# First cross attention of a decoder kernel: value products with queries on partitions, sums in two columns of ones, division there, weighted rows turned on TensorE

## The reference, cut to what matters

```python
def proj(x, W):
    return (x @ W.T).reshape(b, -1, HEADS, D_K).transpose(0, 2, 1, 3)
qh, kh, vh = (proj(q, Wq), proj(k, Wk), proj(v, Wv))
att = jnp.einsum('bhqd,bhkd->bhqk', qh, kh) / jnp.sqrt(jnp.float32(D_K))
att = jnp.where(mask, NEG, att)
att = jax.nn.softmax(att, axis=-1)
out = jnp.einsum('bhqk,bhkd->bhqd', att, vh)
out = out.transpose(0, 2, 1, 3).reshape(b, -1, D_MODEL)
return out @ Wo.T
```

## Time and profile before

| | us |
|---|---|
| median of 3 runs | 2332.08 (2328.46 to 2333.09) |
| profiled execution | 2333.0 |
| its span | 2331.2 |
| mean granted TensorE clock | 0.955 |
| TensorE matmul busy | 2144.7 (92%) |
| TensorE weight load busy | 1749.1 (75%) |
| VectorE busy | 1134.2 (49%) |
| ScalarE busy | 974.6 (42%) |
| POOL busy | 662.4 (28%) |

### The profile page before, as it was taken

One profiled execution on the slowest core, in us unless ns is written; L12 is line 12 of the kernel. 1 busy time (PEld: TensorE's weight loads), 2 busy tenths in 40 slices (PEclk: granted clock), 3 DMA queues, 4 the chain that ended last, 5 costly groups with the idle time before them and its releaser, 6 DMA issues. The chain is left out here.

```text
span 2331.2 us, 41914 instructions
## 1 busy us (share of the span) xinstructions
PE 2144.7 (92%) x13788; PEld 1749.1 (75%) x13789; DVE 1134.2 (49%) x3298; ACT 974.6 (42%) x1907; POOL 662.4 (28%) x889
## 2 busy tenths in 40 slices
PE   7997898779999789999998699889999999999998
PEld 5664455468999656666665477789899999999997
DVE  4543786755333477777765255354222222222245
ACT  2221564343444345555555233301455555555310
POOL 1111777662601234444422122127000000000063
PEclk9997999889999969999999799799999999999999
DMA  9940000033222322222221100155111111011033
GB/s 310 386 158 1 1 1 28 23 101 116 71 70 86 86 92 92 93 93 92 92 74 38 57 4 5 61 193 174 36 34 34 35 32 36 32 36 32 28 116 100
DMA packets 153119, 183.46 MB, mean 79 GB/s; under 512 B 27602, under 2 KB 121362, under 8 KB 152850
## 3 DMA queue, kind: packets, MB, share of 16 engines
q1 hardware_dynamic: 137730, 145.34, 19.2%
q0 software_dynamic: 12288, 33.57, 4.6%
q10 hardware_dynamic: 2960, 2.75, 0.5%
HBM read 73.34 MB, written 74.19 MB: 63 GB/s over the span
## 5 line engine op out<-in xcount | busy, mean ns | idle before, releaser
L2578 DVE CUSTOM_DVE_ANT_0 a_s_ps<-a_s_ps,a_causal 128x512 f32<-128x512 f32 (+3 forms) x512 | 242.2, 512 | 118.0 <-PE a_s_ps L2368 116.3
L2501 ACT ACTIVATE a_prob<-a_st_ps 128x512 f32<-128x512 f32 (+1 forms) x384 | 197.1, 526 | 200.3 <-PE a_st_ps L2384 195.1
L2024 PE MATMUL e_up_ps<-e_xT,e_ring 128*128 128x128 f32 x2272 | 276.7, 275 | 0.0
L2024 PEld LDWEIGHTS e_up_ps<-e_xT,e_ring 128*128 128x128 f32 x2272 | 270.7, 192 | 3.8
L1976 POOL DMA_INDIRECT e_wgu<-slots_y,slot x64 | 61.2, 957 | 620.3 <-DMA slots_y<-e_y 575.8
L2059 ACT ACTIVATE e_hT<-e_up_ps 128x512 f32<-128x512 f32 x103 | 61.5, 597 | 370.5 <-PE e_y_ps L2034 363.0
L2054 ACT ACTIVATE e_ring<-e_wgu 128x512 f32 (+2 forms) x355 | 180.8, 531 | 77.6 <-PE e_up_ps L2024 75.9
L2034 PE MATMUL e_y_ps<-e_wd,e_hT 128*128 x852 | 195.7, 379 | 0.0
L2384 PE MATMUL a_st_ps<-rf_qs,a_ks 128*128 128x512 f32 (+3 forms) x512 | 179.6, 394 | 4.7 <-DMA rf_qs<-a_m_lo 3.2
L2368 PE MATMUL a_s_ps<-a_ks,rf_qs 68*128 68x512 f32 (+3 forms) x512 | 158.3, 354 | 24.0 <-DVE a_most L2578 23.3
L2292 POOL TENSOR_SCALAR_AFFINE_SELECT a_prob<-a_prob 128x256 f32<-128x256 f32 x256 | 98.5, 410 | 285.9 <-ACT a_prob L2501 285.7
(11 more groups left out here) (453 smaller groups left out, 4041.8 us busy)
## 6 DMA issues: line engine op xcount, KB each, us to landing
slots_x<-zero_row SPq DMA_DIRECT2D x4, 8448.0 KB, 50.0
e_xin<-slots_x SPq DMA_DIRECT2D x142, 128.0 KB, 2.0
rf_qs<-late_w SPq DMA_DIRECT2D x128, 128.0 KB, 2.4
a_ks<-late_w SPq DMA_DIRECT2D x120, 128.0 KB, 2.3
slots_x<-e_y SPq DMA_DIRECT2D x71, 128.0 KB, 1.7
slots_y<-e_y SPq DMA_DIRECT2D x71, 128.0 KB, 1.7
e_wgu<-in_L_ffn_wg SPq DMA_DIRECT2D x8, 688.0 KB, 9.8
e_wgu<-in_L_ffn_wu SPq DMA_DIRECT2D x8, 688.0 KB, 11.2
```

The costliest lines, as they stand in the source:

```text
L2024: last = pe.matmul(up_ps[:, j, bank, (first + n) * P:(first + n + 1) * P], weights, xT[:, j, k * P:(k + 1) * P], start=k == 0, stop=k == K ...
L2501: act.activation(prob[:, n % 2, u // 3, (u % 3) * BANK:(u % 3) * BANK + cols], st_ps[:, u % 2, 0:cols], ACT.Exp).then_inc(exp_done, 1)
L2578: last = dve.tensor_tensor_reduce(s_ps[:, u % 2, off:off + cols], s_ps[:, u % 2, off:off + cols], causal[:, S - cols:], 1.0, -3.0e38, ALU. ...
```

## The change

The value products change sides. The turned probabilities of a pair of heads (128 keys by 128 queries) are held in the array, and `vblk` moves: 32 columns of values and two more, one column of ones for each head of the pair (zeros at the other head's keys). The result has queries on partitions, and for each pair 32 weighted values and 2 sums. VectorE takes the reciprocal of the 16 sums and multiplies the 256 values by them (`shared`). TensorE then transposes the 256 columns in two pieces (`turn_out`), ScalarE copies them as before, and the projection follows. Gone are the sum over the probabilities (L1178) and POOL's pass over them (L931); `turn_probs` waits for the exponentials alone. The projection is a step later, of tile i - 5, and stands ahead of the turning of probabilities; on VectorE the maximum stands ahead of `shared(i - 4)` and the addition to x. POOL sets the columns of ones once.

The diff, with a few declarations left out:

```diff
@@ sizes and buffers
-        o_half = lambda i: out_bank[:, 0, 0:D].rearrange("p (k q) -> p k q", k=KT)
+        PAIR = 2 * HD + 2
+        o_pairs = out_bank[:, 0, 0:PAIRS * PAIR].rearrange("p (n c) -> p n c", n=PAIRS)
         w_half = lambda i: out_bank[:, 1, 0:D]
+        turned_half = out_bank[:, 1, D:2 * D]
-        vblk = sb("vblk", [P, 2, PAIRS, 2 * HD])
+        vblk = sb("vblk", [P, 2, PAIRS, PAIR])
+        share = sb("share", [P, 2, PAIRS, 2])
+        o_rows = sb("o_rows", [P, 2, D])
@@ POOL
-            def normalise(i):
-                pool.wait_ge(share_done, i + 1)
-                pool.tensor_tensor(heads(i), heads(i), share[:, i % RING].unsqueeze(2).broadcast_to([P, HEADS, SC]),
-                                   ALU.mult).then_inc(prob_done, 1)
+            pool.memset(vblk[:, :, :, 2 * HD:PAIR], 0.0).then_inc(ones_ready, 1)
+            pool.wait_ge(ones_ready, 1)
+            pool.memset(vblk[0:SC, :, :, 2 * HD:2 * HD + 1], 1.0).then_inc(ones_ready, 1)
+            pool.wait_ge(ones_ready, 2)
+            pool.memset(vblk[SC:P, :, :, 2 * HD + 1:PAIR], 1.0).then_inc(ones_ready, 1)
+            pool.wait_ge(ones_ready, 3)
             for i in range(STEPS):
                 if tile(i):
                     subtract(i)
-                if tile(i - 1):
-                    normalise(i - 1)
@@ TensorE
             def turn_probs(i):
-                pe.wait_ge(prob_done, i + 1)
+                pe.wait_ge(exp_done, i + 1)
...
             def weighted(i):
                 pe.wait_ge(p_kept, i + 1)
                 pe.wait_ge(v_kept, i // TB + 1)
-                after(pe, o_kept, i)
+                after(pe, o_shared, i)
+                if i == 0:
+                    pe.wait_ge(ones_ready, 3)
                 for n in range(PAIRS):
-                    r = 2 * HD * (n % 4)
-                    last = pe.matmul(o_half(i)[r:r + 2 * HD, n // 4, :], vblk[:, i // TB % 2, n, :], probT[:, i % 2, n, :], start=True, stop=True)
+                    last = pe.matmul(o_pairs[:, n, :], probT[:, i % 2, n, :], vblk[:, i // TB % 2, n, :], start=True, stop=True)
                 last.then_inc(o_done, 1)
+
+            def turn_out(i):
+                pe.wait_ge(o_shared, i + 1)
+                after(pe, x_done, i)
+                for k in range(KT):
+                    last = pe.transpose(turned_half[:, k * P:(k + 1) * P], o_rows[:, i % 2, k * P:(k + 1) * P], g.ident[:, :])
+                last.then_inc(o_turned, 1)

             def project_out(i):
                 pe.wait_ge(o_kept, i + 1)
-                after(pe, x_done, i)
@@ TensorE's loop
                 if tile(i + 1):
                     scores(i + 1)
+                if tile(i - 5):
+                    project_out(i - 5)
                 if tile(i - 2):
                     turn_probs(i - 2)
...
                 if tile(i - 3):
                     weighted(i - 3)
                 if tile(i - 4):
-                    project_out(i - 4)
+                    turn_out(i - 4)
...
+            project_out(NT - 1)
@@ ScalarE
             def keep_weighted(i):
-                act.wait_ge(o_done, i + 1)
-                after(act, w_done, i - 1)
-                act.activation(oT[:, i % 2], o_half(i), ACT.Copy).then_inc(o_kept, 1)
+                act.wait_ge(o_turned, i + 1)
+                act.activation(oT[:, i % 2], turned_half.rearrange("p (k q) -> p k q", k=KT), ACT.Copy).then_inc(o_kept, 1)
-                if tile(i - 3):
-                    keep_weighted(i - 3)
+                if tile(i - 4):
+                    keep_weighted(i - 4)
@@ VectorE
-            def shares(i):
-                dve.wait_ge(exp_done, i + 1)
-                dve.tensor_reduce(total[:, i % RING], heads(i), AX.X, ALU.add).then_inc(sum_done, 1)
-                dve.wait_ge(sum_done, i + 1)
-                after(dve, prob_done, i + 1 - RING)
-                dve.reciprocal(share[:, i % RING], total[:, i % RING]).then_inc(share_done, 1)
+            def shared(i):
+                dve.wait_ge(o_done, i + 1)
+                dve.reciprocal(share[:, i % 2], o_pairs[:, :, 2 * HD:PAIR]).then_inc(share_done, 1)
+                dve.wait_ge(share_done, i + 1)
+                after(dve, o_turned, i - 1)
+                dve.tensor_tensor(o_rows[:, i % 2].rearrange("p (n a c) -> p n a c", n=PAIRS, a=2),
+                                  o_pairs[:, :, 0:2 * HD].rearrange("p n (a c) -> p n a c", a=2),
+                                  share[:, i % 2].unsqueeze(3).broadcast_to([P, PAIRS, 2, HD]), ALU.mult).then_inc(o_shared, 1)
@@ VectorE's loop
                 if tile(i):
                     masked(i)
+                if tile(i):
+                    maximum(i)
+                if tile(i - 4):
+                    shared(i - 4)
                 if tile(i - 5):
                     add_to_x(i - 5)
-                if tile(i):
-                    maximum(i)
...
-                if tile(i - 1):
-                    shares(i - 1)
```

More of the change, by code:

```diff
@@ L840, in l0_cross_attention @@
         gate, gate_bias, sorted_ = routing.gate, routing.gate_bias, routing.sorted
-        most, total, share = (sb(n, [P, RING, HEADS]) for n in ("most", "total", "share"))
+        most = sb("most", [P, RING, HEADS])
+        share = sb("share", [P, 2, PAIRS, 2])
+        o_rows = sb("o_rows", [P, 2, D])
         probT = sb("probT", [P, 2, PAIRS, P])
@@ L1185, in keep_value @@
                 after(dve, o_done, (c - 1) * TB)
-                dve.tensor_tensor(vblk[:, c % 2], seq_bank[:, 0:D].rearrange("p (n c) -> p n c", n=PAIRS),
+                dve.tensor_tensor(vblk[:, c % 2, :, 0:2 * HD], seq_bank[:, 0:D].rearrange("p (n c) -> p n c", n=PAIRS),
                                   head_of_key[:, :].unsqueeze(1).broadcast_to([P, PAIRS, 2 * HD]), ALU.mult).then_inc(v_kept, 1)
```

5 lines of the change are left out of this document (3 added, 2 removed).

## The result

| | before | after |
|---|---|---|
| median (executions) | 2330.59 (6) | 2352.39 (6) |
| lowest to highest | 2322.82 to 2333.09 | 2342.61 to 2355.43 |
| profiled execution, its span | 2333.0, 2331.2 | 2353.8, 2351.6 |
| stage, from the start of step 0 to its last row | 268.3 | 288.4 |

The changed kernel is slower: the ratio is 1.0092, with a 95% interval of 1.0068 to 1.0115. The forecast was 2351.0, within 2338 to 2366.

A forecast was written before the change was run, and what follows sets the result against it. TensorE's queue was taken as the bound in steps 4 to 19, POOL in 20 to 26, VectorE's routing chain at the end. Eight window terms summed to +19.2 us on the median 2332.08, giving 2351, range 2338 to 2366.

The forecast's parts named there:

- The price of the products: Value products on TensorE: sixteen instructions with 128 columns held take 1.70 us instead of 0.58, +1.12 us a tile.
- A microsecond added to it there is a microsecond of the span: Steps 4 to 19: TensorE is the bound as a queue of work, so work added there lengthens the span equally.
- Steps 4 to 7: Window of four loop steps: 25.35 us goes to 30.4, with waits left in its first and last step; +5.1 us.
- Steps 8 to 11 and 20 to 23: Two windows: 5.4 us more TensorE work each, plus waits; in the second, POOL waits mostly go; +4.9 and +2.3 us.
- Steps 12 to 15: Window of four loop steps: 25.35 us plus 5.4 of work and 1.4 of waits make 32.1; +5.8 us.
- The halved clock behind that wait stays: Steps 16 to 19: TensorE's half clock behind the routing count's wait was to remain; the window was put at +4.7 us.
- POOL's bound in steps 20 to 26: POOL is the bound there, one tile taking 7.5 us; without the dividing pass, steps 24 to 27 shorten by 4.3 us.
- Two sums leave that chain early: Steps 28 to 35, set by VectorE's routing chain: 2.7 us leave it, 2.3 come back at the end; -0.4 us.
- Faster: Rival: dividing pass and sum were the bound, new products cost like today's; -11.7 us, 2320; 7%.
- Half hidden: Rival: VectorE's relief also shortens the end by 6 us, or the half clock doesn't return in count steps; 2341; 11%.
- Dearer products: Rival: each load of 128 columns waits for the 34 moving ones ahead, 14 us; 2365; 7%.
- a new loop: Rival: with one product bank, tile i-3 waits for VectorE's division of tile i-4, 1 us in 25 steps; 2376; 4%.

The follow-up runs named there:

- the twelve transposes: The kernel before with 12 transposes of the identity matrix added ahead of each tile's value products, nothing else of the change; 2353.93 us, ratio 1.0104.
- e6: The kernel with both parts: the kernel before without sum, reciprocal and POOL's dividing pass, plus twelve more transposes a tile on TensorE; 2332.2 us, ratio 1.0.
- e2: The kernel before without the sum over the probabilities, its reciprocal and POOL's dividing pass, so weights are not normalised; 2303.46 us, ratio 0.9897.
- e10: The changed kernel with four more identity transposes a tile on TensorE, ahead of the value products; 2361.63 us, ratio 1.0126 to the kernel before.
- e11: e6 with its twelve added transposes replaced by seven products of 34 moving columns (14 instructions); 2347.74 us, ratio 1.0067 to the kernel before.

## Why the prediction was right, point by point

The total was forecast at +19.2 us in the profiled execution and measured at +20.8 (2333.0 to 2353.8), of which the stage is 20.1.

| steps | forecast | measured |
|---|---|---|
| 0 to 3 | +1.1 | +1.0 |
| 4 to 7 | +5.1 | +3.8 |
| 8 to 11 | +4.9 | +4.2 |
| 12 to 15 | +5.8 | +6.8 |
| 16 to 19 | +4.7 | +5.1 |
| 20 to 23 | +2.3 | +1.6 |
| 24 to 27 | -4.3 | -4.4 |
| 28 to 35 | -0.4 | +2.0 |

- **The price of the products** was right: 1.70 us a tile, +1.12, shown by the timeline and, at full clock, by issuing them twice (51.6 us for 54). The transposes took 0.26 instead of 0.22, a term mis-sized by 1 us in all.
- **"A microsecond added to it there is a microsecond of the span"** held to six tenths or more in steps 4 to 19: the twelve transposes, 5.6 us in four steps, gave 4.5, 3.7, 4.8 and 3.5 us. The rest went into the small waits.
- **Steps 4 to 7** were 1.3 us too dear, and 1.0 of it is a slip in the sum. With the projection a step later, this window has three projections and not four (12 instructions of L1059 in the trace, 16 of L1047 before), and the last window has nine and not eight (36 and 32). The forecast added the 0.97 us at the end and did not take it off here.
- **Steps 8 to 11 and 20 to 23** were 0.7 us too dear each. The waits came out as forecast (1.15 us in both, for 1.1 and 1.2). TensorE's busy time grew by 4.7 us instead of 5.4. Why is open.
- **Steps 12 to 15** were 1.0 us too cheap. The row after stands at clock 0.95, 3.3 us at the half clock, which the forecast had at none.
- **Steps 16 to 19** were 0.4 us too cheap. "The halved clock behind that wait stays" did not hold: it went from 7.0 to 10.4 us, which costs 1.7. So work and waits together were 1.3 too dear here.
- **POOL's bound in steps 20 to 26** went as forecast: no wait for it at the turns, and steps 24 to 27 shorter by 4.4 us. The size is partly luck: the forecast took these steps at full clock, and 6.7 us of them still stand at the half clock. In steps 8 to 15 TensorE is 96% busy, as asked for.
- **"Two sums leave that chain early ... the added products, turn and projection at the end give 2.3 back: -0.4"** is the step that failed, by 2.4 us. At full clock these steps went from 47.6 to 46.3 by the estimate, which is near it. But the time at the half clock rose from 20.9 to 27.6 us in these steps, 3.4 us lost. A value product group that started at the half clock there takes 3.47 us, as TensorE's timeline of after shows twice:

```profile
490.55 3.47 PE L1046 MATMUL c_out<-c_vblk,c_probT 128*128 128x34 f32 x16
...
504.73 3.47 PE L1046 MATMUL c_out<-c_vblk,c_probT 128*128 128x34 f32 x16
```

- **The rivals.** "Faster" fell with 1.70 us for the products. "Half hidden" (2341) fell, since the end became no shorter. "Dearer products" fell in the timeline and with 62 columns, "a new loop" in the waits: no wait of the products for the division is among the changed kernel's.
- **What was right by luck.** The mechanism holds: TensorE's queue pays for the added rows. But the sum had no term for the clock apart from the late turns. Work less holes gave +12 to +15 us and the clock +5 to +8. Terms that were too dear by about as much covered what was left out, and so the total met. The kernel with both parts shows how far that could have gone: about the same work and relief with less clock lost is no slower than before.

## What to carry to other kernels

Price a product that is turned around by its held side: with 128 columns held, sixteen float32 instructions cost 1.70 to 1.73 us with 8, 34 or 62 columns moving, and where 32 are held and 128 move they cost 0.58. Relief for other engines counts only in the stages where TensorE has holes; in a full queue it gave 0.0 us. And read the granted clock beside each window on both sides. Two kernels with about the same work in the stage (e6 and the changed one) took the same time at full clock and differed by 17 us through the clock. It should be a term of the forecast with a range of its own. Where the clock of every execution is known, take the mean over them: a single profile misled here three times (e2, e10, e11).

## What the runs showed of the hardware that was not expected

- VectorE's reciprocal goes by elements and is dear: 0.25 us for 16 elements a partition and 1.75 for 256, where a multiplication of 256 takes 0.42.
- Small VectorE operations between SBUF tiles were lengthened while a POOL pass over 1024 columns ran. One copy of six numbers (L773 before) took 3.4 us, and 0.33 in the kernel after. The three multiplications of 64 columns in L641 took 1.30 us on the mean and 0.22 after. With the dividing pass and the sum taken out (e2), one pass of 1.9 us was still running beside that copy, and it took 1.43. In the kernel before two passes stood there, and the copy ended with the second. That POOL's passes are the cause is read from these timelines and was not tried by itself.
- The part of the span behind the stage, which no kernel changed, was 1827 to 1841 us long in the profiled executions. A difference of 5 us between two profiles says nothing unless the stage itself shows it.
